# Layer-0 preparation with its transfers in another order, the second routing in pieces, and part of layer 1's start placed in layer 0's last super

## The chip, the cores and the metric

The kernel runs on one core of one Trainium2 chip. The metric is device time in microseconds of one execution. Inside a core five engines work side by side, each with its own instruction stream: TensorE (PE, matrix products), VectorE (DVE), ScalarE (ACT), GpSimd (POOL) and SyncE (SP, which here only issues transfers). They wait for each other through semaphores. Transfers (DMA) are issued from SP, ACT and POOL.

## What is computed

`x` has 32 sequences of 64 tokens with 512 features: 2048 tokens. Two layers follow each other, each with a residual sum:

```python
# layer 0: per-sequence 64x64 matrix, then a feed-forward layer with per-token low-rank experts (top 2 of 8)
h = einsum('bct,bcd->bdt', x, L0_cond_weights[itok])
probs = softmax(h @ W_r.T + b_r);  w_topk, idx = top_k(probs, 2)
base1 = h @ W1.T + b1;  u1 = einsum('nd,erd->ner', h, A1)
for k in range(2):
    z1 = u1 masked to expert idx[:, k]
    a  = gelu(base1 + z1 @ B1 * 2)
    z2 = einsum('nf,erf->ner', a, A2) masked to expert idx[:, k]
    x += w_topk[:, k] * (a @ W2.T + b2 + z2 @ B2 * 2)
# layer 1: per-sequence 64x64 matrix and bias, then routed experts (top 2 of 8) and a shared expert
h = einsum('bct,bcd->bdt', x, L1_cond_weights[itok2]) + side
x += routed_experts(h, top_k(softmax(h @ gate_w), 2)) + silu(h @ sw_gate) * (h @ sw_up) @ sw_down
```

## The kernel before

All large products are made from numbers split into a rounded high half and a low half (`_hi`, `_lo`): hi*hi, hi*lo and lo*hi, so each product is three matmuls. Usually ScalarE casts the high half and VectorE or POOL subtracts it to get the low half. The order of work on every engine is written out by hand; semaphores with constant counts tie the streams together. Buffers of different stages lie over each other in SBUF, so part of the waits guard a region and not a value.

**Layer 0, preparation.** The tokens are cut into 4 "supers" of 512. For each, the per-sequence matrices are gathered into block-diagonal tiles `bd` (`load_block`: 64x64 blocks, one DMA each, shared out over SP, POOL and ACT), `cond_x` multiplies, `high_x` and `low_x` split the result (`xt_hi`, `xt_lo`). `router_and_u1` makes router logits and low-rank products; `logits_and_u1` (ACT) copies them out, `logit_rows` (PE) transposes the logits. `route(k)` (DVE) does softmax and top 2 for supers 2k and 2k+1, some 30 small instructions in a chain. The ratios of the two weights (`rho`) are transposed, copied by ACT (`rho_rows`), stored to DRAM as `wrow_d` and read back spread over all partitions as `wb`, super by super; the first step of the main work on VectorE multiplies by `wb`. The transposed x of supers 2 and 3 is stored to DRAM (`xt_hi_d`, `xt_lo_d`, 4 MB) since its place belongs to W2 later.

**Layer 0, main loop.** For each super, 16 tiles of the hidden width. A step is `hidden` (14 matmuls), `down` of the tile before in two halves (8 + 8) and `second` (2). For tile i, ACT applies `gelu_first` and `gelu_second`, and DVE's `hidden_tile` makes g_hi and g_lo from them (6 instructions). In super 0 the W1 and W2 tiles come raw (`load_w1` into `w_raw`), are split by `high_w1`, `high_w2` (ACT), `low_w1` (POOL), `low_w2` (DVE), and the split W1 is stored (`store_w1`, `w1s_d`) for the later supers (`load_w1s`). At a super's end `low_rank` (DVE), `sums_end` (PE) and `add_sums` (DVE) finish the sums; `store_x1` writes x1 to DRAM.

**The join.** After super 3 all engines meet at a barrier (`l0_over`, count 5; `through` leaves and waits, `leave` only leaves), since layer 1's buffers lie over layer 0's. Behind it come `rows_step(0, k)` for k = 0 to 5, for the first super of layer 1: 0 and 1 multiply by the gathered matrices (`bdq`, `acc`) and add the bias into `xc`; 2 and 3 transpose `xc` in ps_u and split it; 4 and 5 make gate logits. The shared expert's weights come in pieces (`load_s`, POOL's queue) and are split by `high_s` (ACT) and a low half that DVE (pieces 0 and 2) and POOL (the others) make. `gate_up_shared(s, q)` runs 6 tiles per super, the short tile (12 matmuls) first, the others with 24; `rows_step(s + 1, ...)` is woven in between. `keep_warm` issues bf16 matmuls without a use. Then the routed experts run over 39 slot tiles with gathers and scatter-adds on POOL's queue; nothing is edited there.

## Time and profile before

| | |
|---|---|
| median of 3 runs | 1071.82 us (1070.95 to 1079.04) |
| profiled execution | 1073.18 us, its span 1071.6 us |
| TensorE busy | 1020.5 us, 95% of the span |
| VectorE, ScalarE, POOL busy | 534.3, 314.1, 352.1 us |
| TensorE's mean granted clock | 0.987 of 2.4 GHz |
| preparation of layer 0 | 0 to about 65 us |
| main loop of layer 0 | to 537 us |
| join, shared expert | to about 780 us |
| routed experts | to the end |

The rows of the section further down are of two kinds. A timeline row has the start and the duration in us, the engine (a "q" behind it means its queue of transfers), the line, the operation with output <- inputs, how many were merged, and in brackets how long the engine was idle just before and who released it. A window row has the busy time of each engine in a stretch. Matmul rows overlap: a row of 0.39 us is followed by the next start 0.23 us later, so times of several matmuls are read from start to start.

### The profile page before, as it was taken

The numbers are of one execution on the slowest core, as the hardware profiler recorded it, in microseconds if no ns is written. First come the engines' busy times: TensorE is split into PE (matmuls) and PEld (weight loads), VectorE is DVE, ScalarE is ACT, GpSimd is POOL, SyncE is SP. The second block draws the span as 40 slices with busy tenths as digits, with TensorE's granted clock in tenths as the row PEclk, the third lists the DMA queues.
The fourth block names the chain that finished last, engine by engine and source line by source line (L and its number), as shares of the span: only waits on it lengthen the run. The fifth ranks groups of instructions, "written<-read, shape, count | busy, mean of one in ns | idle before, by whom it ended". The sixth has DMA issues, their size and how long they took to land.

```text
span 1071.6 us, 14937 instructions
## 1 busy us (share of the span) xinstructions
PE 1020.5 (95%) x4922; PEld 840.5 (78%) x4923; DVE 534.3 (50%) x888; ACT 314.1 (29%) x548; POOL 352.1 (33%) x349
## 2 busy tenths in 40 slices
PE   7879999999999999999978999999999999999993
PEld 5658887888888888788845778778879999998993
DVE  3678776545474545554475443484553324452100
ACT  3543332121122112111123110210035445444551
POOL 3123345420000000000024000003058888898874
PEclk9989999999999999999999999999999999999997
DMA  6567553444343434432237110101446555556432
GB/s 202 222 214 229 163 167 116 143 156 142 115 128 130 154 115 162 148 137 84 104 134 237 39 40 1 40 1 50 169 160 157 154 157 119 149 119 159 77 61 39
DMA packets 51371, 136.42 MB, mean 127 GB/s; under 512 B 8788, under 2 KB 10052, under 8 KB 50820
## 3 DMA queue, kind: packets, MB, share of 16 engines
q1 hardware_dynamic: 37540, 109.51, 29.8%
q0 software_dynamic: 12368, 25.68, 11.7%
q10 hardware_dynamic: 1424, 0.75, 0.3%
q8 instruction: 19, 0.31, 0.1%
q14 instruction: 20, 0.16, 0.0%
HBM read 96.85 MB, written 39.07 MB: 127 GB/s over the span
## 4 chain that ended last, share of the span: by engine, by line
PE 80%; DMA 5%; DVE 5%; POOL 4%; issue 2%; ACT 1%; SPq 1%; PEldq 0%; POOLq 0%; DVEq 0%; PEld 0%; ACTq 0%
PE ps_y L1605 5%; PE ps_y L1607 5%; PE ps_y L1606 5%; PE ps_h L1565 5%; PE ps_h L1564 5%; PE ps_h L1563 5%; DMA out_x<-yt,slot_tok 3%; PE ps_u L1618 3%; PE ps_u L1617 3%; PE ps_y L1766 2%; PE ps_h L1837 2%; PE ps_y L1767 2%; PE ps_y L1837 2%; PE ps_y L1832 2%; PE ps_y L1833 2%
## 5 line engine op out<-in xcount | busy, mean ns | idle before, releaser
L1153 DVE TENSOR_TENSOR h<-h,wb 128x512 f32<-128x512 f32 x64 | 44.3, 692 | 175.9 <-ACT h L871 169.9
L865 ACT ACTIVATE h<-ps_h,bias 128x512 f32<-128x512 f32 x64 | 44.0, 689 | 237.3 <-PE ps_h L1572 234.2
L1605 PE MATMUL ps_y<-w_hi,g_hi 128*128 (+1 forms) x256 | 102.7, 401 | 1.4 <-DVE g_lo L1161 1.4
L1607 PE MATMUL ps_y<-w_hi,g_lo 128*128 (+1 forms) x256 | 101.9, 398 | 0.0
L1606 PE MATMUL ps_y<-w_lo,g_hi 128*128 (+1 forms) x256 | 101.7, 397 | 0.0
L1563 PE MATMUL ps_h<-xt_hi,w_hl 128*128 128x512 f32 x256 | 100.0, 391 | 0.7 <-ACT lg_t L827 0.7
L1565 PE MATMUL ps_h<-xt_hi,w_hl 128*128 128x512 f32 x256 | 100.3, 392 | 0.0
L1564 PE MATMUL ps_h<-xt_lo,w_hl 128*128 128x512 f32 x256 | 100.2, 391 | 0.0
L1385 DVE CAST eg_hi<-e_raw 128x704 fp32r<-128x704 f32 x32 | 19.9, 683 | 127.9 <-PE ps_y L1862 117.0
L871 ACT ACTIVATE h<-ps_h,bias 128x512 f32<-128x512 f32 x64 | 43.9, 688 | 114.8 <-PE ps_h L1585 114.8
L739 POOL DMA_INDIRECT out_x<-yt,slot_tok x39 | 63.2, 1620 | 24.3 <-DMA out_x<-yt,slot_tok 12.1
L671 POOL DMA_DIRECT2D s_raw<-in_sgu x8 | 4.3, 548 | 196.7 <-DVE g_lo L1161 192.1
L745 POOL TENSOR_TENSOR xg_lo<-xg_f,xg_hi 128x512 fp32r<-128x512 f32 x39 | 58.1, 1490 | 15.1 <-ACT xg_f L971 13.4
L1605 PEld LDWEIGHTS ps_y<-w_hi,g_hi 128*128 128x128 f32 x256 | 48.5, 189 | 13.3 <-issue 1.4
L1607 PEld LDWEIGHTS ps_y<-w_hi,g_lo 128*128 128x128 f32 x256 | 48.5, 189 | 11.8
L1563 PEld LDWEIGHTS ps_h<-xt_hi,w_hl 128*128 128x128 f32 x256 | 48.1, 188 | 12.2 <-ACT lg_t L827 1.2
L1606 PEld LDWEIGHTS ps_y<-w_lo,g_hi 128*128 128x128 f32 x256 | 48.6, 190 | 11.4
L1564 PEld LDWEIGHTS ps_h<-xt_lo,w_hl 128*128 128x128 f32 x256 | 48.1, 188 | 11.1
L1166 DVE TENSOR_TENSOR g_lo<-h,g_hi 128x512 fp32r<-128x512 f32 x64 | 55.6, 869 | 2.2
L1565 PEld LDWEIGHTS ps_h<-xt_hi,w_hl 128*128 128x128 f32 x256 | 48.1, 188 | 10.4
L757 POOL TENSOR_TENSOR rgt_lo<-rgt_f,rgt_hi 128x384 fp32r<-128x384 f32 x39 | 53.7, 1376 | 5.4 <-ACT rgt_f L989 5.4
L1832 PE MATMUL ps_h<-eg_hi,xg_hi 128*128 x156 | 50.9, 327 | 2.7 <-ACT xg_hi L968 1.8
(312 smaller groups left out, 2475.8 us busy)
## 6 DMA issues: line engine op xcount, KB each, us to landing
...
x_in<-in_x SPq DMA_DIRECT2D x4, 1024.0 KB, 6.3
...
x_d<-xres SPq DMA_DIRECT2D x4, 1024.0 KB, 7.7
acc<-x_d SPq DMA_DIRECT2D x4, 1024.0 KB, 7.8
```

The source lines that it names most:

```text
L739: pool.indirect_dma_start(out=out, in_=yt[t % 4][:], in_offset=None, out_offset=bass.IndirectOffsetOnAxis(ap=slot_tok[:, t:t + 1], axis=0) ...
L745: nc.gpsimd.tensor_tensor(xg_lo[:].rearrange("p c n -> p (c n)"), xg_f[:], xg_hi[:].rearrange("p c n -> p (c n)").bitcast(F32), ALU.subtract)\
L757: nc.gpsimd.tensor_tensor(rgt_lo[:].rearrange("p c n -> p (c n)"), rgt_f[:], rgt_hi[:].rearrange("p c n -> p (c n)").bitcast(F32), ALU.sub ...
L1153: tt(h1[u][:], h1[u][:], wb[:, v, :], ALU.mult).then_inc(gch, 1)
L1166: tt(g1_lo[u][:], h1[u][:], g1_hi[u][:].bitcast(F32), ALU.subtract).then_inc(g1_done, 1)
L1563: mm(ps_h[:, u, :], w_chunk(u, 0, c), xt_hi[v][:, c, :], start=(c == 0), stop=False)
L1564: mm(ps_h[:, u, :], w_chunk(u, 0, c), xt_lo[v][:, c, :], start=False, stop=False)
L1565: mm(ps_h[:, u, :], w_chunk(u, 1, c), xt_hi[v][:, c, :], start=False, stop=False)
L1605: mm(ps_y[:, j, :], g_hi[u][:, cols], sl(w2_hi), start=first, **kw)
L1606: mm(ps_y[:, j, :], g_hi[u][:, cols], sl(w2_lo), start=False, **kw)
L1607: mm(ps_y[:, j, :], g_lo[u][:, cols], sl(w2_hi), start=False, **kw)
L1832: mm(o, xg_hi[:, c, :], w(eg_hi, c), start=(c == 0), stop=False)
```

## The change

It has four parts.

1. *Gathers.* For super 1, SP loads two blocks instead of four (`load_bd`), POOL the other two as well.
2. *Transfers.* The ratios' store (`wrow_d`) and the first `wb` are issued by ACT, around `masks(0)` and ahead of the first gelus, with a wait for the store between them. On SP, both `store_w1` and `load_w1(2)`, `load_w1(3)` go ahead of the four stores of transposed x.
3. *Second routing.* `route` is taken apart. `logits_below_max(1)` runs behind tile 0, `choice(1, 0)` behind tile 1, `choice(1, 1)` and `ratios(1)` behind tile 2. ACT's `exps(1)` moves ahead of `high_w2(3)`.
4. *Join.* In super 3, SP loads `acc` 0 and 1 behind tiles 3 and 7, with the gate weights. DVE makes the diagonals, splits the gate and adds the bias rows between tiles; ACT makes `high_s` 0, 1, 2 behind tiles 12, 14 and 15, POOL all four `low_s` (DVE none). PE's row products (`cond_rows`, into ps_h) stand two ahead of the last `down` and two behind it; DVE and ACT read two each (`take_x`). `rows_step(0, 2)` and `(0, 3)` use four banks (`turn_bank`) and come with `sums_end` ahead of the barrier. `rows_step(0, 4)` stands behind it, `rows_step(0, 5)` behind the first shared tile, on DVE behind that tile's products. `store_x1(3)` is cut into 4 pieces. A filler of 72 numbers per partition is added to the layout, and `u1t` moves.

The core of the diff:

```diff
@@ SP
             def load_bd(n):
-                for j in range(TPS // 2 if n == 2 else TPS):
+                for j in range(TPS // 2 if n in (1, 2) else TPS):
-            for n in range(2, NS):
-                sp.wait_ge(xt_lo_done, 4 + (n + 1) * DC)
-                for half, dst in zip(xt_of(n), (xt_hi_d, xt_lo_d)):
-                    sp.dma_start(dst[n - 2], ...)
...
-            sp.wait_ge(wt_sb, 1)
-            sp.dma_start(wrow_d[0:J // 2, :], rho_t[0][:]).then_inc(wrow_st, 16)
+            for f in range(2):
+                store_w1(f)
+            load_w1(2)
+            load_w1(3)
+            for n in range(2, NS):
+                sp.wait_ge(xt_lo_done, 4 + (n + 1) * DC)
+                for half, dst in zip(xt_of(n), (xt_hi_d, xt_lo_d)):
+                    sp.dma_start(dst[n - 2], ...)
             sp.wait_ge(wrow_st, 16)
-            load_weights(0)
-            for f in range(2):
-                load_w1(f + 2)
-                store_w1(f)
             load_weights(1)
...
+                    if s == NS - 1 and f in (TPS, 2 * TPS):
+                        sp.wait_ge(d_done, 2 + s * FT + f)
+                        load_acc(f // TPS - 1)
@@ POOL, behind load_s(0), load_s(1)
-            through(pool, l0_over, 5)
+            leave(pool, l0_over)
+            for n in range(DC):
+                if n == 0:
+                    pool.wait_ge(z_ok, 2 * NS)
+                elif n == 1:
+                    pool.wait_ge(a_done, STEPS)
+                elif n == 2:
+                    pool.wait_ge(z_done, 2 + STEPS)
+                else:
+                    pool.wait_ge(ech, 4 * (NS - 1) + 2)
+                low_s(n, sg_lo_done[n % 2])
+                pool.wait_ge(sg_lo_done[n % 2], n // 2 + 1)
+                load_s(n + 2)
+            pool.wait_ge(l0_over, 5)
@@ ACT
             rho_rows(0)
+            act.wait_ge(wt_sb, 1)
+            act.dma_start(wrow_d[0:J // 2, :], rho_t[0][:]).then_inc(wrow_st, 16)
             masks(0)
+            act.wait_ge(wrow_st, 16)
+            act.dma_start(wb[:, 0, :], wrow_d[0:TPS, :]...).then_inc(wb_in[0], 16)
             act.wait_ge(warm, 1)
...
+                    if s == NS - 1 and f in (FT - 4, FT - 2, FT - 1):
+                        high_s((FT - 4, FT - 2, FT - 1).index(f))
+            nc.scalar.activation(c1["m"][:], zero16[:, 0:J], ACT.Silu)
+            take_x(2)
+            take_x(3)
+            high_s(3)
@@ DVE, super 0
+                            logits_below_max(1)
...
-                        if f == 1:
-                            route(1)
+                        if f in (1, 2):
+                            choice(1, f - 1)
+                        if f == 2:
+                            ratios(1)
@@ DVE, super 3 and behind
+                    if s + 1 == NS:
+                        split_gate()
+                        bias_rows(s)
+                        for u in range(2):
+                            hidden_tile(s * FT + FT - 2 + u, v, u)
+                        take_x(0)
+                        take_x(1)
...
                     dve.wait_ge(mul_done, i + 1)
+                    if i == 0:
+                        rows_step(0, 5)
+                        dve.wait_ge(x1_st, X1_STORED)
```

SP's queue at the start, behind the last gather, before (xt are the stores of transposed x, `wrow_d` the ratios' store, `w1s_d` the stores of split W1, `w_raw` the loads of weight tiles):

```order
L499 DMA xt_hi_d<-w_hi 128x2048 [waits xt_lo_done]
L499 DMA xt_lo_d<-w_hi 128x2048
L499 DMA xt_hi_d<-w_lo 128x2048 [waits xt_lo_done]
L499 DMA xt_lo_d<-w_lo 128x2048
L527 DMA wrow_d<-rho_t 8x128 [waits wt_sb]
L469 DMA wb<-wrow_d 128x512 [waits wrow_st]
L466 DMA w_raw<-in_w1b 128x1216 [waits w2_lo_done,w1_lo_done]
L503 DMA w1s_d<-w_hl 128x1408 [waits w1_lo_done]
L466 DMA w_raw<-in_w1b 128x1216 [waits w2_lo_done,w1_lo_done]
L503 DMA w1s_d<-w_hl 128x1408 [waits w1_lo_done]
L469 DMA wb<-wrow_d 128x512
```

and in the changed kernel:

```order
L505 DMA w1s_d<-w_hl 128x1408 [waits w1_lo_done] x2
L472 DMA w_raw<-in_w1b 128x1216 [waits w2_lo_done,w1_lo_done] x2
L537 DMA xt_hi_d<-w_hi 128x2048 [waits xt_lo_done]
L537 DMA xt_lo_d<-w_hi 128x2048
L537 DMA xt_hi_d<-w_lo 128x2048 [waits xt_lo_done]
L537 DMA xt_lo_d<-w_lo 128x2048
L475 DMA wb<-wrow_d 128x512 [waits wrow_st]
```

The ratios' store and the first `wb` have left SP, the wait for the ratios stands last, and both stores of split W1 stand first.

TensorE at the join, from the end of the last `down` to the barrier, before (`zero` is `keep_warm`, L1633 is the first row of `sums_end`, L1712 the row products, L1720 the transposes of xc):

```order
L1617 MATMUL ps_u<-g_hi,w_hl 128x512 [waits g1_done]
L1618 MATMUL ps_u<-g_lo,w_hl 128x512
L1492 MATMUL ps_h<-zero 128x512 x12
L1633 MATMUL ps_y<-b2s_hi,z_hi 128x512 [waits z2_ok]
...
L1712 MATMUL ps_u<-acc,bdq 128x512 [waits bdq_done,acc_in0,l0_over]
L1712 MATMUL ps_u<-acc,bdq 128x512
```

and in the changed kernel, the same stretch up to the barrier and then the end of the first shared tile with what follows it (L1770 are the row products of the next super):

```order
L1669 MATMUL ps_u<-g_hi,w_hl 128x512 [waits g1_done]
L1670 MATMUL ps_u<-g_lo,w_hl 128x512
L1697 MATMUL ps_h<-acc,bdq 128x512 [waits xc_done]
L1697 MATMUL ps_h<-acc,bdq 128x512
L1780 MATMUL ps_u<-ident,xc 128x128 [waits ech,xc_done]
...
L1812 MATMUL ps_h<-xs_hi,sg_lo 128x512
L1794 MATMUL ps_u<-ident,lgt 128x16 [waits lgt1_cp]
L1794 MATMUL ps_u<-ident,lgt 128x16 x3
L1770 MATMUL ps_u<-acc,bdq 128x512 [waits lg1_read,bdq_done,acc_in1]
```

Two of the four row products (the other two stand ahead of that `down`) and the transposes now stand ahead of `sums_end`; the row products of the next super stand right behind the transposes of logits, with a wait for `lg1_read`.

POOL in super 3, in the changed kernel (before, the first low half stood behind the `iota` that waits for `l0_over`):

```order
L699 TENSOR_TENSOR sg_lo<-s_raw,sg_hi 128x1408 [waits s_hi_done,z_ok]
L680 DMA s_raw<-in_sgu 128x704 [waits sg_lo_done0]
L680 DMA s_raw<-in_sgu 128x704
L699 TENSOR_TENSOR sg_lo<-s_raw,sg_hi 128x1408 [waits s_hi_done,a_done]
L680 DMA s_raw<-in_sgu 128x704 [waits sg_lo_done1]
L680 DMA s_raw<-in_sgu 128x704
L699 TENSOR_TENSOR sg_lo<-s_raw,sg_hi 128x1408 [waits s_hi_done,z_done]
```

Four low halves stand there (the fourth not shown), ahead of the barrier; they wait for ACT's casts and for regions of layer 0 to come free.

## Rows read from the trace of the kernel before

**Rows 1.** Windows: busy us (x count) by engine, TensorE clock, DMA share, GB/s.
```profile
40.00:60.00 20.00, 12.10 (x67) 8.92 (x66) 11.62 (x26) 8.26 (x14) 1.62 (x2) 0.86 0.69 260
200.00:500.00 300.00, 299.64 (x1303) 243.07 (x1302) 162.95 (x277) 58.18 (x86) 15.40 (x30) 1.00 0.40 135
```

**Rows 2.** Timeline of TensorE, start: start, us, operation, [idle before <-releaser].
```profile
17.87 3.84 PE L1512 MATMUL ps_y<-bd,x_in 128*128 128x128 f32 x32 [2.85 <-DMA bd<-in_cond]
...
58.96 0.60 PE L1484 MATMUL ps_u<-ident,lg_t 16*128 16x16 f32 x4 [7.90 <-ACT lg_t L827]
59.49 0.80 PE L1605 MATMUL ps_y<-w_hi,g_hi 128*128 128x512 f32 x1
...
65.58 0.39 PE L1563 MATMUL ps_h<-xt_hi,w_hl 128*128 128x512 f32 x1
...
77.88 0.50 PE L1605 MATMUL ps_y<-w_hi,g_hi 128*128 x1 [1.03 <-DVE g_lo L1161]
```

**Rows 3.** Timeline of SP, start: DMA issues.
```profile
9.00 0.66 SPq L455 DMA_DIRECT2D x_in<-in_x  x1
...
42.41 0.33 SPq L527 DMA_DIRECT2D wrow_d<-rho_t  x1
49.29 0.34 SPq L469 DMA_DIRECT2D wb<-wrow_d  x1
...
50.15 0.43 SPq L503 DMA_DIRECT2D w1s_d<-w_hl  x1
```

**Rows 4.** Timeline of ScalarE, start.
```profile
48.78 1.27 ACT L871 ACTIVATE h<-ps_h,bias 128x512 f32<-128x512 f32 x2 [1.00 <-PE ps_h L1585]
57.52 0.78 ACT L816 CAST w_hl<-w_raw 128x704 fp32r<-128x704 f32 x1 [7.48 <-DMA w1s_d<-w_hl]
```

**Rows 5.** Timeline of VectorE, start.
```profile
42.13 1.29 DVE L1131 TENSOR_TENSOR w_lo<-w_raw,w_hi 128x512 fp32r<-128x512 f32 x2
...
54.23 0.69 DVE L1153 TENSOR_TENSOR h<-h,wb 128x512 f32<-128x512 f32 x1 [5.89 <-DMA wb<-wrow_d]
...
56.28 0.69 DVE L1161 TENSOR_TENSOR g_lo<-h,g_hi 128x512 fp32r<-128x512 f32 x1
```

**Rows 6.** DMA issues by line: count, size, median us to landing.
```profile
x_in<-in_x SPq DMA_DIRECT2D x4, 1024.0 KB, 6.3
...
side_col<-in_side POOLq DMA_DIRECT2D x32, 0.2 KB, 2.3
```

**Rows 7.** Timeline of TensorE, join of the layers.
```profile
537.13 1.90 PE L1492 MATMUL ps_h<-zero 128*128 128x512 bf16 x8
...
549.46 1.96 PE L1712 MATMUL ps_u<-acc,bdq 128*128 128x512 f32 x4 [0.26 <-PEq L367]
...
559.98 1.94 PE L1720 MATMUL ps_u<-ident,xc 128*128 128x128 f32 x8 [3.34 <-DVE xs_lo L1271]
...
571.01 1.88 PE L1712 MATMUL ps_u<-acc,bdq 128*128 128x512 f32 x4
...
581.71 0.79 PE L1750 MATMUL ps_h<-xs_hi,sg_hi 128*128 128x512 f32 x1
```

**Rows 8.** Timeline of ScalarE, join.
```profile
535.46 0.69 ACT L871 ACTIVATE h<-ps_h,bias 128x512 f32<-128x512 f32 x1 [1.64 <-PE ps_h L1585]
549.29 2.63 ACT L918 CAST sg_hi<-s_raw 128x1408 fp32r<-128x1408 f32 x2 [13.14 <-PEq L367]
```

**Rows 9.** Timeline of VectorE, join.
```profile
573.79 0.69 DVE L1428 TENSOR_TENSOR sh_g<-sh_s,ps_h 64x512 f32<-64x512 f32 x1
...
579.42 1.41 DVE L1264 TENSOR_SCALAR xc<-ps_u,side_col 128x512 f32<-128x512 f32 x2 [1.99 <-DMA xc_d<-xc]
```

**Rows 10.** Timelines of POOL and VectorE: tensor_tensor side by side, and POOL's widest.
```profile
84.11 1.75 POOL L653 TENSOR_TENSOR w_hl<-w_raw,w_hl 128x640 fp32r<-128x640 f32 x1
...
84.47 1.95 DVE L1166 TENSOR_TENSOR g_lo<-h,g_hi 128x512 fp32r<-128x512 f32 x1
...
566.85 3.20 POOL L700 TENSOR_TENSOR sg_lo<-s_raw,sg_hi 128x1408 fp32r<-128x1408 f32 x1
```

266 lines of the change are left out of this document (144 added, 122 removed).

## The prediction

> **What bounds the kernel now.** Read the stretches first: in the middle of layer 0 TensorE is busy 299.64 of 300 us with 1303 matmuls [rows 1], 0.230 us each. A step of the layer-0 loop, 32 matmuls, is 7.39 us. Whatever moves the end there must remove TensorE work, and the change removes none. So I looked for places where TensorE does not run, in TensorE's own order of time: there are two, the start and the join of the layers, and they are the two that are edited.
>
> The start: TensorE waits 2.85 us for gathered condition blocks before super 1 [rows 2]. Later it stops for 7.90 us, until 58.96, for ScalarE's copy of the last router logits; the 16 matmuls of the first `down` then take 65.58 - 59.49 = 6.09 us, not 3.7, because the clock was let down in the hole (40 to 60: 0.86) [rows 1, 2]. Why was ScalarE late? Its cast of W1 tile 2, ahead of that copy, waited 7.48 us for the store `w1s_d` [rows 4], which SP issued only at 50.15, behind the wait for the 4 KB transfer of the routing ratios: issued at 42.41, next row issued at 49.29 [rows 3]. VectorE was late for the same reason: `wb`, issued at 49.29, released it at 54.23, and its g_lo ended at 56.97 [rows 5].
>
> The join: from the end of the last layer-0 loop (537.13, `keep_warm` x8) to the third shared tile (581.71) TensorE needs 44.58 us [rows 7] for about 30 us of work.
>
> **Part 1, block gathers.** SP issues two of super 1's blocks less, POOL two more. The hole is 2.85 us; the x tile of the same super, issued at 9.00 and 6.3 to land [rows 3, 6], comes at 15.3 instead of the blocks' 17.87, so 2.3 us can go (bounds 0 and 2.85). Everything up to the logits follows, since this stretch runs hand over hand; POOL's last blocks come 2.3 us later, where they have some 3 us in hand.
>
> **Part 2, reordered transfers.** The ratios' store and `wb` go to ScalarE's queue; SP's 4 MB of transposed x go behind both W1 stores and two W1 loads. New times, by the 2.3 us of part 1: ratios issued at 40.2. How long they take on a queue with nothing ahead is not shown; bounds are 2.3 us (a 0.2 KB transfer, `side_col` [rows 6]) and 6.9 (now [rows 3]). I take 2.6, nearer the small one, as the long one had 2 MB issued just ahead on its queue. So they land at 42.8. This matters twice, because ScalarE now waits for them ahead of its gelus, and TensorE's `second` waits for those. The gelus are due at 46.51 - 2.3 = 44.2, so the wait is covered by 1.4 us. `wb` is issued at 43.0; it took 4.9 (49.29 to 54.2 [rows 3, 5]) and now has 4 MB beside it: I take 6 (bounds 4.9 and 9.8, twice as long), landing 49.0. The first g_lo ends 2.74 us later (54.23 to 56.97 [rows 5]), at 51.8. ScalarE's cast no longer waits for a store and needs `w_raw` 2, issued at 42.8 - 2.3 = 40.5 [rows 5] and hidden by then: cast and logits' copy end at 49.3 (gelus end 50.05 - 2.3 = 47.8, then 0.78 and 0.58). So VectorE's chain is late next, and `down` starts at 51.8 instead of 59.49: **-7.7** (part 1 is in it). A hole of 2.2 us instead of 7.9 gives the clock back (behind the 2.85 us hole 32 small matmuls took 3.84 us, no slow stretch [rows 2]): 6.09 - 3.7 = **-2.4**.
>
> The Trainium skill (DMA: Bandwidth & Descriptors, Issuing engines are not separate DMA queues) says that issuing from several engines saves only the issuing time, as all run on the same 16 DMA engines. By that rule, read strictly, the ratios take 6.9 us as now; no row here shows a small transfer on ScalarE's queue under this load. This is rival 1.
>
> **Part 3, second routing in pieces.** 30 small VectorE instructions come apart. Today they delay tile 2 and open a hole of 1.03 us [rows 2]. With the earlier start W1's low halves on POOL fall on VectorE's tiles in another phase, so I count 0 (-1 to +1).
>
> **Part 4, join.** The price of the moved parts, in order from the loop's end. TensorE work: 4 warm matmuls and two fp32 row products (0.9 + 1.8, from 1.96 with tail [rows 7]) run until 2.7. But `down` 63 needs g_lo of tile 63. This is where the change hurts: POOL's low halves (3.2 us each on 128x1408 [rows 10]) now run inside layer 0's last super. At 84.1 one can see what that does: a 1.75 us POOL tensor_tensor stretched VectorE's g_lo to 1.95, so that it ended 0.56 after POOL's [rows 10]. Gelu 63 ends at 536.15, ScalarE's new cast (2.63 / 2 [rows 8]) at 537.5; POOL's third low half then holds VectorE's cast from 537.8 to 541.0, and g_lo ends at 541.9, that is 4.8 after the loop's end. The fp32 products hide the first 2.7 of it. Without the lock it would be 2.7.
>
> The Trainium skill (SBUF — State Buffer, Who interferes with whom) has this as an exclusive lock on a shared port pair, held for a whole instruction. The trace agrees (1.95 for 0.69 [rows 10]); by the page a tensor copy from PSUM is untouched.
>
> Then: `down` 63, 16 matmuls, 3.7; two row products 1.8; wait for ScalarE's two reads 1.0; transposes without the wait for low halves 1.9; the low-rank sums, 12 matmuls, 2.8; barrier 0.4; logits, 8, 1.9; shared tile 0, 12, 2.8; transposes of logits 0.4. Next TensorE needs `lg1_read` for its rows step. VectorE does that copy now only behind the products of shared tile 0, which before ended 574.48 - 571.01 = 3.5 after the tile [rows 7, 9]; plus 0.2 copy, less 0.4: a new wait of 3.3. Then row products 1.4, tile 1 (24) 5.6, row products 1.4. Here TensorE waited 1.95 for VectorE, released at 579.42 by the store of xc [rows 9]; xc is stored some 12 us earlier, the wait goes. Sum: 4.8+3.7+1.8+1.0+1.9+2.8+0.4+1.9+2.8+0.4+3.3+1.4+5.6+1.4 = 33.2, against 44.6: **-11.4**.
>
> Against it: the first low half, on POOL after gelu 60 and a cast (tile 60's cast waits 3.1 us. From the start of the second gelu TensorE has 22 matmuls, 5.1 us, until it asks for g_lo; gelu 0.7 and VectorE 2.7 leave 1.7 to spare): 3.1 - 1.7, **+1.5** (0 to 2). The second falls in VectorE's idle time: 0. And a 3.3 us hole: behind today's 3.34 us hole 8 transposes took 1.94 [rows 7], where 8 of the 32 small ones above took 0.96; with some more lost behind them **+1.4** (0 to 2.4, the price at 59.49). The loads of 2 MB of x1 inside the last super lie beside loads of W1 with a full step in hand: 0. Bias rows (2.7 us) and gate split go into 3.7 us of VectorE's idle time: 0. VectorE's own two low halves lie in the old 44.58 and are not counted again.
>
> **Sum.** -7.7 - 2.4 - 11.4 + 1.5 + 1.4 = -18.6 us. The profiled execution spans 1071.6 and took 1073.18 in all; the median of three runs is 1071.82, so I move that: 1053.2, say **1053**. Behind the join the order is as before; the routed stage, paced by POOL and its scatters, may give or take 2.
>
> **The rivals.**
> Rival 1 (0.17): the ratios need 6.9 us though they left SP's queue, since all queues share 16 busy DMA engines. ScalarE, which stands in front of them, starts its gelus at 47.6 instead of 44.2, `wb` lands near 53, g_lo ends at 55.7: 3.8 instead of 7.7, and the longer hole (about 4 us more) keeps the clock's 2.4: 1053.2 + 3.9 + 2.4 = 1059.5. For it: 6.3 us even for an x tile of 1 MB [rows 6]. Against it: the row ahead on the same queue.
> Rival 2 (0.17): POOL's low halves do not hit VectorE's tiles, because ScalarE's casts shift them: 2.1 + 1.5 less, and perhaps `wb` in 4.7 (1.3 less): 1053.2 - 4.9 = 1048.3.
> Rival 3 (0.08): the join's gain is mostly eaten: a chain in my list is missed (VectorE's xc, or the stores of x1 in four pieces ahead of 512 KB of zeros), so that the third shared tile comes only 3 us earlier: 1061.5 to 1063, no change within 1%.
> Rival 4 (0.04), slower: the clock. With several short holes in 25 us it could stay at 1.2 GHz, where a matmul took 0.43 instead of 0.23 us (as behind 58.96 [rows 2]). It costs 0.2 us per matmul, so the 18.6 us are gone after 93 matmuls, three tiles of the shared stage, and 150 slow ones give 1065, 250 give 1085. Against it: behind every hole of today it came back within some 5 us.
> That the change does nothing would need the wait of 7.90 to stay; its releaser is removed by the order itself, so this has no chance of its own.
>
> **How the numbers follow.** My forecast has 0.54. Its own span is given by `wb` (-1.3 to +3), the lock (-3.6 to +1), the clock behind the new wait (-1.4 to +1), part 3 (-1 to +1): together 1049 to 1058. With rivals 1 and 2 the range is **1046 to 1061**, leaving out rivals 3 and 4 and little of the tails. About 1% (10.7 us) is what a measurement of this kernel can tell from no change, so faster is below 1061: forecast, rivals 1 and 2, 0.88; same 0.09; slower 0.03.
>
> **What would show it.** Right if TensorE's idle row before the last `logit_rows` is 1 to 3 us, with the first `down` at 50 to 53 and 16 matmuls in 3.7 us; if ScalarE's row of the `wb` transfer comes by 43.5. Right if VectorE's cast or g_lo of tile 63 takes about 3 us beside a POOL low half; if TensorE has a wait near 3 us ahead of the row products that wait for `lg1_read`, and none ahead of the next two. The loop's end should be at 537.1 - 8.6, the third shared tile at 581.7 - 18.6. Wrong if the hole moves to the gelus (rival 1), if `w_hl` loads are waited for in super 3, or if matmuls of 0.43 us go on past one shared tile.

## The result and the profile after

Over eleven runs the changed kernel took 1066.92 us in the median (1060.71 to 1068.7), the kernel before 1072.51 (1070.95 to 1079.04). The ratio is 0.9917, 95% interval 0.9896 to 0.9938: a gain of 0.8%. It is clear of zero, but under the 1% that the prediction took as the least that can be told from no change; 1053 and a range of 1046 to 1061 were predicted. The profiled executions spanned 1066.5 and 1071.6 us, so 5.1 us have to be explained against the 18.6 forecast.

First TensorE's timeline of the changed kernel, cut to the rows with an idle time ahead of them (start, duration, engine, line, operation, in brackets the idle time and what ended it). They answer to [rows 2] and [rows 7].

```profile
17.51 3.84 PE L1564 MATMUL ps_y<-bd,x_in 128*128 128x128 f32 x32 [1.70 <-DMA bd<-in_cond]
...
57.65 0.79 PE L1657 MATMUL ps_y<-w_hi,g_hi 128*128 128x512 f32 x1 [6.23 <-DVE g_lo L1200]
...
516.12 0.50 PE L1657 MATMUL ps_y<-w_hi,g_hi 128*128 x1 [1.44 <-DVE g_lo L1200]
...
540.14 0.51 PE L1657 MATMUL ps_y<-w_hi,g_hi 128*128 128x512 f32 x1 [2.19 <-DVE g_lo L1200]
...
548.18 1.09 PE L1780 MATMUL ps_u<-ident,xc 128*128 128x128 f32 x8 [0.78 <-ACT xc L944]
...
561.61 3.35 PE L1770 MATMUL ps_u<-acc,bdq 128*128 128x512 f32 x4 [3.30 <-DVE lg L1287]
...
710.58 0.50 PE L1826 MATMUL ps_y<-sd_hi,sh_hi 128*128 128x512 f32 x1 [2.09 <-DVE sh_lo L1487]
...
787.50 0.65 PE L1884 MATMUL ps_u<-ident,xg 128*128 128x128 f32 x4 [1.70 <-DMA xg<-xc_d,slot_tok]
...
811.44 0.97 PE L1928 MATMUL ps_y<-ed_hi,rgt_lo 128*128 x3 [1.72 <-POOL rgt_lo L771]
```

Read against before, stretch by stretch: the first `down` starts at 57.65 instead of 59.49, where 51.8 was forecast; the third shared tile starts at 571.60 instead of 581.71, where 563.1 was forecast; and the end comes only 5.1 us earlier, although nothing behind the shared tiles was changed. So the gain is 1.8 us at the first `down`, 3.6 once the slow stretch and a hole at 77.88 are passed, 10.1 at the third shared tile, and half of that is given back later.

The second hole in the chain of waits (start, duration, what was waited for). It answers to [rows 3] and [rows 5]: the ratios and `wb` left SP's queue, and `wb` takes 9.65 us instead of 4.9.

```profile
42.03 3.12 DMA wrow_d<-rho_t
...
45.17 9.65 DMA wb<-wrow_d
...
54.85 0.70 DVE h L1192
```

What lies beside it on SP (timeline of the queue; the duration is that of the issue): two loads of `w_raw` and the four 1 MB stores of transposed x.

```profile
42.52 1.86 SPq L472 DMA_DIRECT2D w_raw<-in_w1b  x2
44.43 0.42 SPq L537 DMA_DIRECT2D xt_hi_d<-w_hi  x1
...
45.97 1.72 SPq L537 DMA_DIRECT2D xt_lo_d<-w_lo  x1
```

The join, VectorE and POOL (timelines): both POOL instructions of 3.2 us hold a cast of VectorE that takes 0.43 us elsewhere.

```profile
511.83 3.43 DVE L1198 CAST g_hi<-h 128x512 fp32r<-128x512 f32 x1
...
535.95 3.42 DVE L1198 CAST g_hi<-h 128x512 fp32r<-128x512 f32 x1
...
511.76 3.21 POOL L699 TENSOR_TENSOR sg_lo<-s_raw,sg_hi 128x1408 fp32r<-128x1408 f32 x1 [95.87 <-ACT sg_hi L887]
...
535.90 3.17 POOL L699 TENSOR_TENSOR sg_lo<-s_raw,sg_hi 128x1408 fp32r<-128x1408 f32 x1
```

And the granted clock by stretches (columns: stretch, length, then busy time and instructions of PE, PEld, DVE, ACT and POOL, clock, DMA share, GB/s). It fell behind the holes at 540 and 710, and also behind those at 561 (four row products in 3.35 us) and 811 (0.96 over 780 to 820). Before, the same wait for `sh_lo` is at 720.56 with a hole of 2.11 us, and the stretch behind it (720 to 740) has 1.00.

```profile
537.00:545.00 8.00, 5.81 (x17) 4.02 (x16) 5.41 (x6) 0.01 (x1) 3.24 (x3) 0.79 0.35 129
...
700.00:720.00 20.00, 17.91 (x72) 14.37 (x71) 13.69 (x39) 1.17 (x2) 5.69 (x3) 0.91 0.00 0
```

### The profile page after: what moved, and what is told of

It is laid out like the page before. It is cut to its first block, busy times and chain, and to the rows that moved or that the text cites. A ratio compares the mean times of both kernels' runs of the same rounds, so it can differ in the third digit from the quotient of the medians.

```text
span 1066.5 us, 14883 instructions
## 1 busy us (share of the span) xinstructions
PE 1018.3 (95%) x4893; PEld 842.1 (79%) x4895; DVE 527.5 (49%) x884; ACT 315.0 (30%) x550; POOL 360.8 (34%) x353
## 4 chain that ended last, share of the span: by engine, by line
PE 81%; POOL 6%; DMA 4%; DVE 3%; issue 2%; ACT 1%; SPq 1%; PEldq 0%; POOLq 0%; PEld 0%; DVEq 0%; ACTq 0%
PE ps_y L1657 6%; PE ps_y L1659 6%; PE ps_y L1658 6%; PE ps_h L1617 5%; PE ps_h L1616 5%; PE ps_h L1615 5%; PE ps_u L1670 3%; PE ps_u L1669 3%; DMA out_x<-yt,slot_tok 2%; PE ps_y L1826 2%; POOL xg_lo L759 2%; PE ps_y L1827 2%; PE ps_h L1810 2%; PE ps_h L1903 2%; PE ps_h L1811 2%
## 5 line engine op out<-in xcount | busy, mean ns | idle before, releaser
L1657 PE MATMUL ps_y<-w_hi,g_hi 128*128 (+1 forms) x256 | 103.2, 403 | 10.2 <-DVE g_lo L1200 10.2
L1450 DVE CAST eg_hi<-e_raw 128x704 fp32r<-128x704 f32 x32 | 17.1, 594 | 136.9 <-PE ps_y L1928 124.5
L1657 PEld LDWEIGHTS ps_y<-w_hi,g_hi 128*128 128x128 f32 x256 | 48.8, 191 | 22.8 <-DVE g_lo L1200 10.1
L1616 PEld LDWEIGHTS ps_h<-xt_lo,w_hl 128*128 128x128 f32 x256 | 48.1, 188 | 11.1
L731 POOL TENSOR_TENSOR oh_vals<-oh_tile,carry 128x640 fp32r<-128x640 f32 x2 | 6.5, 3247 | 139.7 <-DVE oh_tile L1429 139.7
```

The costliest lines, as they stand in the source:

```text
L1616: mm(ps_h[:, u, :], w_chunk(u, 0, c), xt_lo[v][:, c, :], start=False, stop=False)
L1657: mm(ps_y[:, j, :], g_hi[u][:, cols], sl(w2_hi), start=first, **kw)
```

## The parts apart: join alone, transfers alone, gathers taken back

**e1, join only.** SP's order, the ratios' queue, the gathers and the second routing are put back; the join stays new. The core of the edit:

```
+            sp.wait_ge(wt_sb, 1)
+            sp.dma_start(wrow_d[0:J // 2, :], rho_t[0][:]).then_inc(wrow_st, 16)
+            sp.wait_ge(wrow_st, 16)
+            load_weights(0)
-            act.wait_ge(wt_sb, 1)
-            act.dma_start(wrow_d[0:J // 2, :], rho_t[0][:]).then_inc(wrow_st, 16)
```

> The changed kernel with its first three parts taken back: block gathers, SP's order of transfers (ratios and wb on SP behind the 4 MB of x stores), and the second routing as one block are as in the kernel before; only the join is the new one. Theory (the two parts are separate in time and add up): the profile of the changed kernel has 3.6 us gained by tile 60 of layer 0's last super and 6.5 between there and the third shared tile, 5 of which are lost again later. Without the preparation the first down is back at 59.5 us, tile 60's first gelu at about 511, the third shared tile at 571.6 + 3.6 = 575.2, and the time is 1066.9 + 3.6 = 1070.5, or, where the later loss came only with the earlier start, 1065. Rival (the preparation gains nothing in the end): 1067, as the changed kernel. Rival (the join gains nothing in the end): 1072 or more.

Measured: 1074.41 us (1071.78 to 1075.42), ratio 1.0001 (0.998 to 1.0022); span 1073.2. The new join alone gains nothing at the end. In its trace the wait for `sh_lo` in the shared stage comes at 715.37 instead of 720.56, and 1.0 us later at the start than before, so the join did win 6.2 us. It lost 1.6 behind that wait (slow clock), and the routed stage needed 5.2 us more (294.8 instead of 289.6). Of the three theories the last held (the join gains nothing in the end), the other two fell.

**e12, transfers only.** The kernel before with the first two parts, in the main:

```
-                for j in range(TPS // 2 if n == 2 else TPS):
+                for j in range(TPS // 2 if n in (1, 2) else TPS):
...
+            act.wait_ge(wrow_st, 16)
+            act.dma_start(wb[:, 0, :], wrow_d[0:TPS, :].rearrange("(o j) p -> o (j p)", o=1).partition_broadcast(P))\
+                .then_inc(wb_in[0], 16)
```

> The kernel before with the first two parts of the change only (block gathers, order of the transfers); second routing and join as before. Theory (the parts add up; the join alone was worth nothing, so all of the change's gain is in the transfers): first down at 57.5, wb again 9 to 10 us, the wait for sh_lo in the shared stage 3.6 to 4.5 us earlier than 720.6, the routed stage as before with its fetches at -4 and +19, time 1073 - 4 to 5 = 1068.5. Rival (the join and the preparation help each other): 1071 or more.

Measured: 1069.4 us (1063.61 to 1077.35), ratio 0.9936 (0.9903 to 0.997). First `down` at 56.80, the wait for `sh_lo` at 716.69, 3.9 us earlier than before. The preparation carries most of the change's gain. The hole of 1.03 us at tile 2 is still there (1.04 at 74.46) and is gone in the changed kernel, so it is the second routing in pieces that removes it. But the profile of e12 also lost 4.3 us between slot tiles 5 and 6, with the old join: that loss does not need the join.

**e2, gathers back.** The changed kernel, with the first line pair of e12's edit taken back.

> The changed kernel with only the block gathers of super 1 as before (all four of SP's half issued by SP, none of them by POOL). Theory: part 1 is worth what the idle row before super 1 lost, 0.4 us (17.51 against 17.87) and not the predicted 2.3; here the hole is 2.85 again, super 1 starts at 17.9, wb is issued 0.4 us later, and the time is 1067.3. Rival: the first part is what makes the later transfers collide (POOL's gathers share the 16 DMA engines): then wb lands earlier than 54.8 and the time is 1065 or less.

Measured: 1067.87 us in the median of nine runs, of which one took 2605 us and the others 1066.27 to 1070.16; ratio 0.9944 (0.9919 to 0.997). Super 1 starts at 18.26 with a hole of 3.14 us. Over all profiles super 1 started at 17.87 to 18.30 with the gathers as before (before twice, e1, e2) and at 17.37 to 17.91 with them moved (twelve profiles without added instructions at the very start). Part 1 is worth about half a us. The hole is still ended by `bd`. Which block? In the changed kernel SP's second and last block of super 1, issued at 11.69, has this row (size, us from issue to landing):

```profile
bd<-in_cond SPq DMA_DIRECT2D x1, 16.0 KB, 5.8
```

It lands at 17.47, and super 1 starts at 17.51; POOL's last one, issued at 11.07, lands at 17.22. In all twelve profiles SP's second block is the last to land, 0.05 us ahead of super 1's start. Before, SP's fourth block was issued 2.5 us later (14.17) and landed only 0.35 later (17.82), after 3.7 us. All these blocks were issued behind the 1 MB x tile (9.00, landing at 15.95) and landed only behind it, in the order of their issue. So issuing them earlier bought almost nothing. That the x tile is what holds them is not tested.

## What held wb

**e3.** SP waits for `wb` before it issues the stores of x:

```
+            sp.wait_ge(wb_in[0], 16)
             for n in range(2, NS):
                 sp.wait_ge(xt_lo_done, 4 + (n + 1) * DC)
```

> The changed kernel; SP waits for wb to land before it issues its four 1 MB stores of transposed x. In the changed kernel wb took 9.65 us with those stores issued in the same 1.5 us (44.4 to 46.0). Theory (wb shares the DMA engines with the 4 MB): wb lands in 5 us or less, near 50, the wait of VectorE ends there, the first down starts at 52 to 53 instead of 57.65, the hole is 1 to 2 us instead of 6.2, the clock stays up, and the time is 1067 - 5 - 1.5 = 1060.5. Rival (a transfer of 64 descriptors to all partitions on ScalarE's queue is slow by itself, or the W1 and w_raw loads are what slows it): wb takes 8 us or more again and the time is 1066 to 1068. Rival (the stores come late for what waits on them): the first down is early but the half-way w2 tile waits, and the time is 1063 to 1067.

Measured: 1063.28 us (1062.11 to 1066.36), ratio 0.9893 (0.9856 to 0.993). Chain of waits and first `down` of e3:

```profile
45.43 4.52 DMA wb<-wrow_d
...
51.57 1.58 DVE g_hi L1199
...
53.92 0.51 PE ps_y L1658
```

`wb` (256 KB, a row of 2 KB for every partition) takes 4.52 instead of 9.65 us, on the same queue: the 4 MB beside it had doubled its time. The first `down` starts 3.7 us earlier, the hole is 2.36 instead of 6.23. The cast is 1.58 instead of 0.43 because POOL's low half of W1 (50.85, 2.01 us) now meets it. Slow matmuls (0.43 us each) still came, from 54.8 on, behind 2.36 us of idling. The Trainium skill (DMA: Bandwidth & Descriptors, Issuing engines are not separate DMA queues) says that transfers issued by different engines interleave on the same 16 DMA engines. The trace agrees: 4.52 against 9.65 us on ScalarE's queue, by what SP issued.

## POOL's low halves and the copy of the logits

**e4.** POOL's first and third low half wait for VectorE to finish tiles 60 and 63:

```
-                    pool.wait_ge(z_ok, 2 * NS)
+                    pool.wait_ge(g1_done, STEPS - 1)
...
-                    pool.wait_ge(z_done, 2 + STEPS)
+                    pool.wait_ge(g1_done, 2 + STEPS)
```

> The changed kernel; POOL's first and third low half wait until VectorE has finished tile 60 and tile 63, so that they run in VectorE's idle time. Theory (POOL's 3.2 us instruction holds VectorE's cast, 3.43 instead of 0.43): VectorE's casts of tiles 60 and 63 take 0.43 us, TensorE's idle rows of 1.44 and 2.19 us before downs 60 and 63 go, and so do the slow matmuls (0.43 us each) from 540.5 to 543.8: 1.7 + 2.1 + 1.7 = 5.5 us at the join, time 1061.5. Rival (the casts are slow by themselves or for another reason): still 3.4 us, time 1067. Rival (the last low halves come too late for the first shared tile or the expert loads): a new wait of 1 to 3 us before the shared tiles, time 1063 to 1065.

Measured: 1060.48 us (1056.55 to 1062.58), ratio 0.9861 (0.9812 to 0.9911). VectorE and POOL of e4 at tile 63:

```profile
533.11 0.43 DVE L1198 CAST g_hi<-h 128x512 fp32r<-128x512 f32 x1
...
535.41 3.24 POOL L699 TENSOR_TENSOR sg_lo<-s_raw,sg_hi 128x1408 fp32r<-128x1408 f32 x1 [2.36 <-DVE g_lo L1205]
```

Casts 0.43 us, both TensorE holes gone, the transposes of x at 541.34 instead of 548.18: 6.8 us, of which 1.1 came from the start. 5.7 against 5.5 expected.

**e7.** `rows_step(0, 5)` on VectorE moves ahead of shared tile 0's products:

```
                     i, o = s * SH + q, shared_tile(q)
+                    if i == 0:
+                        rows_step(0, 5)
                     dve.wait_ge(sil_done, i + 1)
...
                     if i == 0:
-                        rows_step(0, 5)
```

> The changed kernel; VectorE makes its copy of the transposed layer-1 logits before the products of shared tile 0 instead of behind the first of them. In the changed kernel TensorE waited 3.30 us for it, and four row products behind the wait took 3.35 us instead of 1.88. Theory (a wait by order, as predicted): the wait falls to 0.3 to 0.6 us, the row products take 1.9 us, the slow clock at 561 goes: 3.0 + 1.5 = 4.5 less up to the third shared tile, time 1062.5. Rival (VectorE's xc sums that follow the row products wait for the store of xc anyway, 1.18 us more now): half of it comes back, time 1064.5. Rival (the gain is eaten behind the shared stage, as the join's own was): 1066 or more.

Measured: 1059.01 us (1058.51 to 1059.86), ratio 0.9851 (0.9816 to 0.9886). TensorE of e7:

```profile
556.04 1.96 PE L1771 MATMUL ps_u<-acc,bdq 128*128 128x512 f32 x4 [0.41 <-DVE lg L1287]
```

The wait is 0.41 instead of 3.30, and the row products take 1.96 instead of 3.35. From the transposes of x to the wait for `sh_lo` e7 needs 158.15 us, the changed kernel 162.40: 4.25, where 4.5 was expected. That e7's profile is 8.4 us shorter has other reasons too, which the edit does not touch: its clock fell neither behind the 2.19 us hole ahead of `down` 63 (1.5 us) nor behind the wait for `sh_lo` (1.6 us), and it was 1.1 us earlier at tile 60.

**e8, the three edits together.**

> The changed kernel with the edits of e3 (x stores behind wb), e4 (POOL's low halves apart from VectorE's last tiles) and e7 (logits copy early) together. Theory (they lie in different stretches and add up to the shared stage): the wait for sh_lo, at 710.6 in the changed kernel, comes 4.4 + 5.5 + 4.5 us earlier, at 696.2; the routed stage takes 293 us or less, and the time is 1052 to 1054. Rival (what is gained ahead of the routed stage is lost in it): 1057 or more.

Measured: 1052.84 us (1050.57 to 1054.46), ratio 0.979 (0.9763 to 0.9818). The wait for `sh_lo` stands at 697.14 (expected 696.2), so the edits add up to within 1 us; span 1052.6. In the same set of runs the unchanged kernel of after took 1065.13 (e6, next section). The routed stage took its part here too.

## Where the rest of the gain went

The routed stage works through slot tiles of 128 rows: POOL gathers the rows of a tile (`xg`), TensorE transposes them and multiplies, and POOL issues a scatter that adds the result to `out_x`. A tile's start is the start of `ps_u<-ident,xg`, and a step is the time from one tile's start to the next one's; tiles count from 0. A second profile of before and of after first, each as it was:

> The kernel before, unchanged, profiled once more. All kernels with the new join show two things in the routed stage that the profile of before did not: a wait of 1.7 to 2.0 us for the gathered rows of slot tile 2 (before: 0.39), and a first scatter that lands late, so that TensorE waits 1.2 to 1.7 us for rgt_lo at slot tile 5. Theory (it is chance in the routed stage, not the change): a second profile of before shows them in part too, or another place of the same size, and its first slot tile starts at 782 again. Rival (the new join causes them): before shows 0.4 and nothing at tile 5 again; its span from the first slot tile to the end is 289.6 again, against 292.9 in the changed kernel.

> The changed kernel, unchanged, profiled and timed once more. Its eleven times stood in two groups, near 1062 and near 1068. Theory (each short hole of TensorE draws a few us of slow clock in some executions and none in others, 1.6 us apiece): the profile again shows the same holes, but a slow stretch behind another choice of them; up to the first slot tile it is the first profile to 2 us, and the times are again 1060 to 1069. Rival (the two groups come from the routed stage, a late scatter or not): with a time near 1062 TensorE's wait for rgt_lo at tile 5 is gone.

Measured: e5 1075.12 us once, span 1073.5; e6 1065.13 us (1061.9 to 1069.27), ratio 0.9909 (0.9877 to 0.994), span 1067.3. First slot tiles, POOL's scatters and SP's weight loads of e5:

```profile
790.14 0.60 PE L1818 MATMUL ps_u<-ident,xg 128*128 128x128 f32 x4
796.76 0.66 PE L1818 MATMUL ps_u<-ident,xg 128*128 128x128 f32 x4 [0.34 <-DMA xg<-xc_d,slot_tok]
...
817.21 0.60 PE L1818 MATMUL ps_u<-ident,xg 128*128 128x128 f32 x4
824.40 0.60 PE L1818 MATMUL ps_u<-ident,xg 128*128 128x128 f32 x4
...
808.81 1.77 POOL L739 DMA_INDIRECT out_x<-yt,slot_tok  x1 [0.30 <-issue]
815.67 1.58 POOL L739 DMA_INDIRECT out_x<-yt,slot_tok  x1 [0.71 <-issue]
...
810.28 0.37 SPq L596 DMA_DIRECT2D e_raw<-in_wgu  x1
```

The same rows of the changed kernel:

```profile
779.51 0.60 PE L1884 MATMUL ps_u<-ident,xg 128*128 128x128 f32 x4
...
807.74 0.60 PE L1884 MATMUL ps_u<-ident,xg 128*128 128x128 f32 x4
...
818.76 0.60 PE L1884 MATMUL ps_u<-ident,xg 128*128 128x128 f32 x4
...
798.98 1.70 POOL L753 DMA_INDIRECT out_x<-yt,slot_tok  x1 [0.30 <-issue]
808.78 1.58 POOL L753 DMA_INDIRECT out_x<-yt,slot_tok  x1 [3.50 <-DMA out_x<-yt,slot_tok]
...
799.78 0.37 SPq L605 DMA_DIRECT2D e_raw<-in_wgu  x1
```

Step 1 to 2 is 8.0 instead of 6.6 us, step 5 to 6 is 11.0 instead of 7.2. Both losses stand in both profiles of after and in neither of before (e6: 8.4 and 11.1; e5: 6.6 and 7.2), so they don't look like chance between two executions. From the first slot tile to the end after needs 292.9 us and e6 295.8, before 289.6 and e5 289.2. What differs at the first one is the queue of instruction fetches. The part on DMA queues for 1.2 us of the changed kernel, just ahead of the gather for tile 2:

```profile
q8 instruction: 1, 0.02, 5.0%
```

One packet of 0.02 MB of code, about 1 us of one of the 16 DMA engines, in the middle of 2 MB of weights. Such packets come every 22 to 35 us in the shared stage, as TensorE works through its code: between those at 687.1 and 720.2 us stand 128 matmuls and 128 weight loads. The change had shortened that code, by the compiled program, from 5019 to 4965 instructions. The packet now comes 8 us behind the first slot tile's start instead of 3 to 4 ahead of it. The Trainium skill (Runtime: NRT & Kernel Launch, Instruction fetch mechanics) says code is refilled in blocks of 16 KiB, 256 instructions, by DMA, at a cost that is mostly hidden. The packet's size (16384 bytes in the trace) and the 256 instructions agree. What it costs the transfers beside it is tested here.

The landings show where the delay arises. In after the last weight load ahead of the gather (192 KB) takes 10.2 us from issue to landing and the gather 4.7; before, with the packet elsewhere, they take 8.7 and 3.4. The weight load is late already, so the delay is not the gather's own.

**e9 and e18: 54 instructions more in the changed kernel**, in the hole before the first `down` (two waits make one instruction):

```
                     logit_rows(NS - 1)
+                    for _ in range(108):
+                        pe.wait_ge(z_done, 2)
```

> The changed kernel with 54 more instructions in TensorE's code, each of which waits for something long true, put into the hole of 6 us before the first down. The change had made TensorE's code 54 instructions shorter (5019 to 4965). In all eight kernels with the new join an instruction fetch (one packet of 0.9 to 1.4 us on one of the 16 DMA engines) falls 8 us behind the start of the first slot tile, among the loads of the second expert and just ahead of the gather for slot tile 2, and another 23 us behind it; in both profiles of before they fall 4 to 5 us ahead of it and 19 behind. Theory (the fetches of TensorE's own code fall on the gather and the scatter): the fetches return to -4 and +19, the wait for xg at slot tile 2 falls from 1.7 to 0.4 us, the first scatter lands within 6 to 7 us instead of 9, the wait for rgt_lo at tile 5 and its slow clock go, the step from the start of tile 1 to that of tile 2 is 6.7 us instead of 8.0, that from 5 to 6 is 7.2 instead of 11.0, and the time is 1066.5 - 1.3 - 3.8 = 1061.5. Rival (something else in the new join, the transfers or POOL's program, disturbs the routed stage): the fetches move and the two steps stay 8.0 and 11.0; time 1066 or more.

> The kernel of e9 once more. Theory: with fetches at -4 and +19 its steps at tiles 1 and 5 are 6.6 and 7.3 us again, its profile 1061 to 1064 long; the times again lie at 1062 to 1064 with one or two near 1067. If the fetch falls at +7 in this execution, the steps are 8 and 11 and its time is 1066 to 1069. Rival: a profile with the fetch at -4 and the long steps, or the other way round.

**e10: 202 more in the kernel before**, 80 and 122 at the two places named:

> The kernel before with 202 more instructions in TensorE's code, each waiting for something long true, 80 in its first idle time and 122 in the hole of 7.9 us before the first down. That puts its code into the same place, modulo 256 instructions, as that of the changed kernel (5221 against 4965, 256 apart). Theory: the fetches move from -4 and +19 to +8 and +23 us behind the first slot tile, its steps from tile 1 to 2 and from 5 to 6 become 8.0 and 9 to 11 us instead of 6.7 and 7.2, and the kernel before is 3 to 5 us slower than it was, 1076 to 1078. Rival (the fetches have no part in it): the steps stay 6.7 and 7.2, time 1073. If the added instructions themselves take longer than the two holes, the starts behind them shift, which the first slot tile's start shows (782.0).

Measured: e9 1063.44 us (1062.56 to 1067.59), ratio 0.9899 (0.9869 to 0.9929), span 1061.3; e18 1062.79 (1061.5 to 1069.11), ratio 0.9917 (0.9888 to 0.9946), span 1060.6. e10 1084.69 (1083.2 to 1086.19), ratio 1.0088 (1.006 to 1.0117). TensorE and scatters of e9:

```profile
779.51 0.60 PE L1886 MATMUL ps_u<-ident,xg 128*128 128x128 f32 x4
786.09 0.66 PE L1886 MATMUL ps_u<-ident,xg 128*128 128x128 f32 x4 [0.31 <-DMA xg<-xc_d,slot_tok]
...
806.58 0.60 PE L1886 MATMUL ps_u<-ident,xg 128*128 128x128 f32 x4
813.84 0.60 PE L1886 MATMUL ps_u<-ident,xg 128*128 128x128 f32 x4
...
798.20 1.77 POOL L753 DMA_INDIRECT out_x<-yt,slot_tok  x1 [0.30 <-issue]
805.21 1.58 POOL L753 DMA_INDIRECT out_x<-yt,slot_tok  x1 [0.86 <-issue]
```

and of e10, the kernel before with longer code:

```profile
794.67 0.60 PE L1822 MATMUL ps_u<-ident,xg 128*128 128x128 f32 x4
802.97 0.66 PE L1822 MATMUL ps_u<-ident,xg 128*128 128x128 f32 x4 [2.03 <-DMA xg<-xc_d,slot_tok]
...
828.15 1.47 PE L1866 MATMUL ps_y<-ed_hi,rgt_lo 128*128 x3 [2.95 <-POOL rgt_lo L757]
```

In e9 the fetches are back at -4 and +19 us and the steps at 6.6 and 7.3; in e10 they are at +8 and +24, the steps 8.3 and 11.7. At slot tiles 0 and 1 the first profile of after and e9 stand within 0.01 us of each other, and the end is 5.2 us apart. (e10's added instructions took about 0.1 us each and outlasted their holes: its first slot tile comes at 788.81, 6.8 later. Its routed stage lost a further 4.) By the medians e9 and e18 are 3.5 and 4.1 us faster than after (1.7 and 2.3 than e6), but by the ratios, 0.9899 and 0.9917 against 0.9917 and 0.9909, hardly at all: the gain is shown by the traces and not by the times. Three of e18's seven runs took 1066.5 to 1069.1, where one or two near 1067 were expected.

**e11, e15 to e17: the three edits and the code.** In e11 all 54 instructions stand in e8's 2.3 us hole, in e15 and e17 (one kernel) 30 stand in TensorE's first idle time and 24 in the hole.

> The three edits of e8 and the 54 instructions of e9 together. The hole before the first down is 2.3 us there, so the added instructions may be in the way. Theory: e8's 1052.8 less 5 us in the routed stage, 1048; if the added instructions take more than the 2.3 us (they would need over 43 ns each), some of it is lost at the start and the first down comes later than 53.7. Rival: 1052 or more.

> The three edits of e8 with the 54 instructions once more, now 30 in TensorE's first idle time of 3.2 us and 24 in the hole of 2.3 us before the first down. The runs showed about 0.1 us for each of these instructions (e9: 54 within a hole of 5.6; e10: 80 in 7.3 us, 122 in 10.9), so both places cover them; in e11 all 54 stood in the 2.3 us hole and cost 3.2 us. Theory (the place of TensorE's code decides where its fetches fall): fetches at -4 and +19, steps of tile 1 and 5 of 6.7 and 7.2 us, first down at 53.7 to 54.2, time 1052.8 - 5 = 1048. Rival (in e11 the same count of instructions gave fetches at +7 and +20, so the place is not decided by the count alone): the fetches are at +7 or +8 and the steps 8 and 11, time 1053.

> The kernel of e15 once more. Its profiled execution took 1056.7 us and had its fetches at +7 and +19 and the steps 8.3 and 13.2; its five other executions took 1047.0 to 1049.8. Theory (where the fetch falls is not fixed by the code alone, and the fast executions had it ahead of the first slot tile): a profiled execution of 1047 to 1050 shows fetches at -4 and +19 and the steps 6.7 and 7.2; one of 1055 or more shows +7 and 8. Rival (the fetches have no part in the two groups): a profile near 1048 with the fetch at +7.

Measured: e11 1056.59 us (1049.96 to 1058.09), ratio 0.981 (0.9776 to 0.9844). e15 1049.05 (1047.0 to 1056.66), ratio 0.9752 (0.9727 to 0.9777); e17 1050.18 (1048.91 to 1056.91), ratio 0.9788 (0.9755 to 0.9821). In e11 the instructions outlasted their place: the hole grew from 2.32 to 5.54 us and the first `down` came at 58.49 instead of 53.67; its rival (1052 or more) held. e15's profiled execution was its slowest, with the fetch at +7 and steps 8.3 and 13.2; that of e17, the same kernel, took 1052.9, between the two groups of its expectation, and had the fetch at -3 with steps 6.7 and 9.9:

```profile
765.01 0.60 PE L1890 MATMUL ps_u<-ident,xg 128*128 128x128 f32 x4
771.75 0.66 PE L1890 MATMUL ps_u<-ident,xg 128*128 128x128 f32 x4 [0.46 <-DMA xg<-xc_d,slot_tok]
...
783.87 2.03 POOL L754 DMA_INDIRECT out_x<-yt,slot_tok  x1 [0.31 <-issue]
793.61 1.58 POOL L754 DMA_INDIRECT out_x<-yt,slot_tok  x1 [3.33 <-DMA out_x<-yt,slot_tok]
...
785.00 0.37 SPq L606 DMA_DIRECT2D e_raw<-in_wgu  x1
```

In e15 the last weight load and the gather take 10.6 and 5.1 us to land, in e17 8.7 and 3.5, from the same instructions. So "the count of instructions decides where the fetch falls" is refuted as a rule (e11 and e15 against e9 and e17). The count does place the fetch before it: 25 to 26 us ahead of slot tile 0 in the eleven profiles with the shorter code or e10's padding, 31 to 32 in the other nine. In the eleven the next one always came at +8 or +9; in the nine it came at -3 or -4 in six and at +6 to +8 in three (e11, e15, e16). What decides between these two stays open. What stands is the link between its place and the wait at tile 2:

| profiles | fetch, us from slot tile 0 | step 1 to 2, us |
|---|---|---|
| before, e5, e9, e18, e17 | -3 to -4 | 6.6 to 6.7 |
| e12 | -4 | 7.2 |
| after, e1 to e4, e6 to e8, e10, e11, e13 to e16 | +6 to +9 | 7.7 to 8.6 |

**e13, e14, e16: the second loss.** Each scatter is issued when the one before has landed, and POOL stands in front of it. The loads of the third expert are issued 24.9 to 26.4 us behind slot tile 0. Where the first scatter was issued 1.47 us ahead of them (before, e5, e9, e18), the second followed 6.9 to 7.0 us later; where it was 1.14 us ahead or less, or behind (thirteen profiles, e12 and e17 among them), 8.9 to 10.8 us. The 1.3 us lost at tile 2 are enough to tip this; in e12 and e17 it tipped without them. The test holds the loads back:

```
                 if e:
                     sp.wait_ge(e_done, e)
+                if e == 2:
+                    sp.wait_ge(y_st, 16)
```

> The changed kernel; SP issues the loads of the third expert's weights only when the first scatter has landed. In all twelve profiles these loads are issued 25 to 26 us behind the first slot tile's start. Where the first scatter was issued at 24.5 us (both profiles of before, e9) the second followed 7 us later; where it was issued at 25.1 us or later (nine profiles, e12 with the old join among them) it followed 9 to 11 us later. Theory (the first scatter and the loads race for the DMA engines; late by half a us, the scatter lies among them): with the loads held back the second scatter follows 7 us behind the first, the wait for rgt_lo at slot tile 5 and its slow clock go, the step from tile 5 to 6 is 7.2 us instead of 11.0, while the wait for xg at tile 2 (8.0) stays; time 1066.5 - 3.8 = 1062.5. Rival (the scatter is late for its own reasons): the second follows 9 us later again and the time is 1066. Rival (the loads are wanted): a new wait for the third expert's halves of 1 to 5 us.

> The three edits of e8 with the loads of the third expert held behind the first scatter as in e13. Theory: e8's 1052.8 less 3.8 us, 1049. Rival (as in e13): 1052 or more.

> The kernel of e15 with the loads of the third expert held back as in e13. Theory: where e15 has its fetches at -4 and +19 there is nothing left for the held load to win, 1048; where it has them at +7, the step from 5 to 6 is 7.2 by the load alone, 1049. Rival: the held load costs more than it wins, 1050 or more.

Measured: e13 1068.8 us (1062.68 to 1073.44), ratio 0.9939 (0.9914 to 0.9964); e14 1057.6 (1052.09 to 1060.68), ratio 0.9829 (0.9798 to 0.9859); e16 1054.65 (1052.76 to 1058.84), ratio 0.9805 (0.9779 to 0.9831). Scatters and the held load of e13:

```profile
796.80 1.70 POOL L755 DMA_INDIRECT out_x<-yt,slot_tok  x1 [0.30 <-issue]
803.50 1.58 POOL L755 DMA_INDIRECT out_x<-yt,slot_tok  x1 [0.30 <-issue]
812.92 1.60 POOL L755 DMA_INDIRECT out_x<-yt,slot_tok  x1 [3.02 <-DMA out_x<-yt,slot_tok]
...
801.88 0.37 SPq L607 DMA_DIRECT2D e_raw<-in_wgu  x1
```

The second scatter now follows after 6.7 us, as the theory said, and step 5 to 6 is 6.8 us. But the load, issued at 801.88, falls on the second scatter, the third comes 9.4 us after it, and two more waits for `rgt_lo` (1.4 and 1.9 us) follow at 844 and 874. The mechanism is shown, the remedy is none: none of the three kernels is faster than without it (e14 against e8: 1057.6 against 1052.8), and e16 is slower than e15 (1054.65 against 1049.05, intervals of the ratios apart). The 3.8 us of the expectation were the price of one collision, and it only moved.

## Why the prediction was wrong, point by point

| step of the prediction | forecast, us | measured in the profile, us |
|---|---|---|
| parts 1 and 2, to the first `down` | -7.7 | -1.8 |
| clock behind that hole, and what follows to tile 60 | -2.4 | -1.8 |
| POOL's first low half | +1.5 | +1.7 |
| join, with its clock | -10.0 | -8.2 |
| all behind the third shared tile | 0 (give or take 2) | +5.0 |
| sum | -18.6 | -5.1 |

Two steps carry the miss: the start, 5.9 us short, and the stages behind the join, 5.0 us.

**Part 2: mis-sized.** "`wb` ... now has 4 MB beside it: I take 6 (bounds 4.9 and 9.8, twice as long)". It took 9.65. The bounds were right, the choice between them was not: the trace put it at the far end. e3 shows the cause, 4.52 us without them. The ratios themselves took 3.1 us (2.6 forecast), so rival 1, ratios that need 6.9, fell; and ScalarE's casts no longer waited, as said. Of the 5.9 us by which the first `down` missed 51.8, `wb` is 3.7, part 1 is 1.8 (ratios issued at 42.03 instead of 40.2) and the ratios are 0.5.

**Part 1: wrong step.** "2.3 us can go" took the x tile as the next thing to be late, once SP issues fewer blocks. The x tile landed at 15.95, but the blocks issued behind it landed only up to 1.5 us later, SP's second one last (17.47): the hole stayed at 1.3 to 3.0 us and the start moved by some 0.5. The step took the time of issue for what makes a block late.

**Clock: wrong.** The hole it was to follow stayed long (6.23), so matmuls of 0.43 us came again behind it, and in e3, with 2.36 us, still. The forecast that a hole of 2.2 us costs nothing came from the stretch behind the 2.85 us hole; e3 and e8 (2.32) had such holes and slow matmuls all the same. The hole of 1.03 us that the second routing opened is gone, where part 3 had counted 0; that made up for part of it, which is luck.

**Join: right in mechanism.** The cast stands beside POOL's third low half as said ("g_lo ends ... 4.8 after the loop's end"): `down` 63 at 540.14, 4.9 behind the loop's end. Wait for ScalarE's reads 0.78 (1.0). New wait for the logits' copy 3.30 (3.3), with 1.5 of slow clock (1.4). No wait ahead of the next row products. Missing was the clock behind the 2.19 us hole of `down` 63, which the same forecast had opened. In nine profiles with this hole the way from `down` 63 to the transposes took either 8.0 us (six, after and e9 among them) or 6.5 (e6, e7, e18): 1.5 us, in six profiles of nine. The rule of an exclusive lock (the Trainium skill, SBUF — State Buffer, Who interferes with whom) fits e4's casts, 0.43 against 3.42 us.

**Behind the join: wrong step.** "Behind the join the order is as before; the routed stage ... may give or take 2." The routed stage took 3.3 more net: 1.3 at tile 2, 3.8 at tile 5, 1.8 given back behind tile 28, where this execution was spared a wait for `rgt_lo` that before had (e6 was not, and took 6.2). The shared stage took 1.6 by slow clock behind the wait for `sh_lo`. In e9, the same kernel with 54 more instructions, the two losses are gone and the routed stage takes 287.6 us instead of 292.9. Rival 2 (no collision with VectorE) and rival 4 (the clock stays down for good) fell. Rival 4's sum is wrong too: 93 slow matmuls cost the 18.6 us, so 150 give 1083 and not 1065. Rival 3 (0.08) had the outcome, no change within 1%, but neither the size (1061.5 to 1063 against 1066.9) nor the cause: the third shared tile came 10.1 us earlier and not 3. The order was indeed as before; the moments of the transfers relative to each other were not.
